# State-space scan with a mixture of experts: tokens routed first, a table of slots instead of sorted rows, experts from tile 8

## What is computed

```python
delta = softplus(xn @ W_delta.T + delta_bias)            # [token, d]
B_sel, C_sel = xn @ W_B.T, xn @ W_C.T                    # [token, d, n], n = 16
A_bar = exp(delta * A);  h = A_bar * h + (A_bar - 1) / A * B_sel * x   # along the 2048 tokens
y = sum over n of h * C_sel
...
scores = xf @ Wr + br                                    # 8 experts, the best 2 of each token
router_weights = softmax over the chosen two
h = gelu(xf @ W1[e] + b1[e]);  y = h @ W2[e] + b2[e]     # hidden size 1024
out = sum over e of router_weights[t, e] * y[e, t]
```

## Time and profile before

| | us |
|---|---|
| median of three runs (1290.12 to 1294.3) | 1290.58 |
| the profiled execution | 1290.72 |
| its span, first to last instruction | 1289.0 |
| prologue, to the start of the scan stage | 103.41 |
| PE / DVE / ACT / POOL busy | 1174.5 / 977.8 / 803.8 / 835.1 |

### The profile page before, as it was taken

One profiled execution on the slowest core, in us unless ns is written; L12 is line 12 of the kernel. 1 busy time (PEld: TensorE's weight loads), 2 busy tenths in 40 slices (PEclk: granted clock), 3 DMA queues, 4 the chain that ended last, 5 costly groups with the idle time before them and its releaser, 6 DMA issues.

```text
span 1289.0 us, 22376 instructions
## 1 busy us (share of the span) xinstructions
PE 1174.5 (91%) x7674; PEld 730.4 (57%) x7674; DVE 977.8 (76%) x1362; ACT 803.8 (62%) x1341; POOL 835.1 (65%) x733
## 2 busy tenths in 40 slices
PE   1467887789899999999999999999999999999996
PEld 0342333455556666666666666666666666666652
DVE  6767998887777777777776866767777776776788
ACT  3553445577788775666567567576756657566631
POOL 2536788357878676665766676666675766667662
PEclk9998989999999999999999999999999999999998
DMA  9942234667768753445344354344444354334423
GB/s 295 301 126 103 80 107 141 229 209 233 260 210 270 235 139 111 119 102 141 104 111 131 93 138 131 90 121 134 105 124 122 100 136 119 107 114 105 103 62 138
DMA packets 87387, 186.96 MB, mean 145 GB/s; under 512 B 12784, under 2 KB 64880, under 8 KB 77168
## 3 DMA queue, kind: packets, MB, share of 16 engines
q1 hardware_dynamic: 59280, 152.80, 35.3%
q0 software_dynamic: 18000, 22.42, 10.6%
q10 hardware_dynamic: 10000, 10.38, 3.3%
HBM read 135.48 MB, written 57.96 MB: 150 GB/s over the span
## 4 chain that ended last, share of the span: by engine, by line
PE 72%; POOL 6%; DVE 6%; issue 5%; ACT 2%; DMA 1%; DVEq 0%; SPq 0%; POOLq 0%; ACTq 0%
PE bank L1165 39%; PE bank L1214 15%; PE bank L1227 15%; POOL xs L953 3%; DVE hb L1069 3%; POOL ax L938 2%; PE bank L1194 1%; PE bank L1239 1%; DVE bank L1047 1%; POOL whl L948 1%; DMA wst<-in_W 1%; DVE bank L1081 1%; PE bank L1246 1%; DVE ysum L1090 1%; DVE bank L1043 0%
## 5 line engine op out<-in xcount | busy, mean ns | idle before, releaser
L938 POOL TENSOR_TENSOR ax<-ax,x 128x512 f32<-128x512 f32 x214 | 272.1, 1279 | 287.2 <-ACT ax L843 285.2
L1165 PE MATMUL bank<-k_xT,k_WB 128*128 128x512 f16 x1536 | 379.5, 384 | 47.2 <-DVE hb L1069 34.4
L1165 PE MATMUL bank<-k_xT,k_WC 128*128 128x512 f16 x1536 | 377.0, 382 | 0.8 <-DVE ysum L1090 0.8
L1047 DVE TENSOR_TENSOR bank<-ax,bank 128x512 f32<-128x512 f32 x214 | 148.4, 693 | 222.9 <-PE bank L1165 197.9
L1165 PEld LDWEIGHTS bank<-k_xT,k_WB 128*128 128x128 f16 x1536 | 146.2, 99 | 200.8 <-DVE hb L1069 51.2
L1165 PEld LDWEIGHTS bank<-k_xT,k_WC 128*128 128x128 f16 x1536 | 151.4, 99 | 186.3 <-issue 7.2
L1069 DVE TENSOR_TENSOR_SCAN hb<-aexp,state,bank 128x512 f32<-128x512 f32 x192 | 244.4, 1273 | 0.0
L833 ACT ACTIVATE aexp<-k_dcur,k_A 128x512 f32<-128x512 f32 x256 | 180.8, 711 | 72.1 <-DVE hb L1069 66.8
L1214 PE MATMUL bank<-xbt,k_x 128*128 128x256 f16 x1872 | 218.7, 274 | 3.8 <-ACT k_x L881 3.8
L1214 PEld LDWEIGHTS bank<-xbt,k_x 128*128 128x128 f16 x1872 | 183.8, 98 | 42.9 <-ACT k_x L881 4.8
L1081 DVE SCALAR_TENSOR_TENSOR bank<-hb,k_rA,bank 128x512 f32<-128x512 f32 x240 | 179.9, 749 | 1.8
(11 more groups left out here) (144 smaller groups left out, 1321.6 us busy)
## 6 DMA issues: line engine op xcount, KB each, us to landing
k_x<-wsplit SPq DMA_DIRECT2D x78, 1024.0 KB, 4.8
wst<-in_W SPq DMA_DIRECT2D x32, 512.0 KB, 5.8
wsplit<-whl SPq DMA_DIRECT2D x32, 512.0 KB, 5.6
xs<-zero ACTq DMA_DIRECT2D x1, 10140.0 KB, 61.1
xb<-xs SPq DMA_DIRECT2D x39, 260.0 KB, 4.5
b<-in_b SPq DMA_DIRECT2D x39, 128.0 KB
k_x<-in_x SPq DMA_DIRECT2D x4, 1024.0 KB, 9.7
stB<-in_WBT SPq DMA_DIRECT2D x8, 512.0 KB, 10.0
```

Of the source, the lines that this page charges most:

```text
L938: nc.gpsimd.tensor_tensor(ax[:, k % MR], ax[:, k % MR], x32[:], ALU.mult).then_inc(ax_done, 1)
L1047: v.tensor_tensor(bank, ax[:, RANK[g] % MR], bank, ALU.mult).then_inc(ux_done, 1)
L1165: ins = mm(bank[:], W[:, a, kc, n, hf * P:(hf + 1) * P], xT[:, c, b, kc, :], start=(k == 1), stop=(k == 3 * KC))
```

## The change

- **Prologue**: unrolled, with x's chunks and the scores first and the weight groups between and after them. The low half of W_B is made by DVE for groups 0, 6 and 7 and by POOL for the others (then ACT needs two operations for W_B, too). Scores of the high and low half of Wr come from one matmul of 16 columns.
- **Slot masks**: a token's slot is split into slot div 128 and slot mod 128. DVE compares both with 0..77 and 0..127 (two operations of 2496 elements per partition, four of 2048), POOL multiplies the first kind by the token's number (two of 2496), and PE multiplies the masks (64 matmuls of 78 columns): the result says which token is in each slot. From it DVE makes `row`, `second` and `target` for all blocks at once.
- **No `xs`**: the zeros and the 64 scatters go. SP writes all normalised rows with two extra columns to `xrows` (4.2 MB, two DMAs) once the gates are known, between weight groups 4 and 5. POOL gathers each block with two indirect DMAs. DVE's `slot_marks` and half of POOL's `slot_data` go.
- **Experts by size**: the experts take their places in order of their number of tokens, so that place p is not needed before block 4p. Two of the 32 weight pieces are split in the prologue, two at tiles 1 and 3, then one in every block.
- **Schedule**: blocks begin at tile 8, four of 7 tiles, then of 6; the last one ends at tile 246 (before: 239). The down product is spread over all tiles of a block from its third on (4 or 5 parts). `DIRECT` is cut to tiles 1, 3, 5, 7. Result rows are added to `acc` after each half of D (15 adds in place of 7), `take_y` of the last block is at tile 252 (before: 244).

In order: the tables of the schedule; in the prologue SP's, ACT's and DVE's programs (the last behind `slotf`); in the scan stage POOL's.

```diff
-E0 = 36
-EARLY, LONG, STEP = E, 6, 5
-DOWN_CUT = (0, 6, 11, 16)
-DIRECT = set(range(1, block_start(EARLY), 2))
-PIECE_AT = {k: E0 - 18 + 4 * k if k < 4 else block_start((k - 4) // 4) + 3 + k % 4 for k in range(SPLITS)}
+E0 = 8
+LONG, STEP, LONGS = 7, 6, 4
+def block_start(b):
+    return E0 + LONG * min(b, LONGS) + STEP * max(b - LONGS, 0)
+def down_steps(b):
+    return list(range(block_start(b + 1) + 2, block_start(b + 2)))
+def down_part(b, k):
+    n = len(down_steps(b))
+    return DOWN[k * len(DOWN) // n:(k + 1) * len(DOWN) // n]
+DIRECT = set(range(1, 8, 2))
+AHEAD = 2
+PIECE_AT = {2: 1, 3: 3, **{k: block_start(k - NPIECE) + 3 for k in range(NPIECE, SPLITS)}}
...
+        for g in range(4):
+            load_group(g)
...
+        load_group(4)
+        sp.wait_ge(meta_set, 1)
+        sp.dma_start(io["xrows"][0:HOLE, :].rearrange("(i p) d -> p i d", p=P),
+                     xall[:, 0:NT // 2, :]).then_inc(keep["rows_out"], 16)
...
+        for g in range(5, NG):
+            load_group(g)
+        sp.wait_ge(order_set, 1)
+        sp.wait_ge(table_made, 1)
+        for k in range(W_BUF):
+            load_piece(sp, io, keep, k)
+        for k in range(AHEAD):
+            store_piece(sp, io, keep, k)
+            load_piece(sp, io, keep, k + W_BUF)
...
-        act.dma_start(io["xs"].rearrange("(p r) d -> p r d", p=P),
-                      zero[:].unsqueeze(1).broadcast_to([P, NSLOT // P, D + META])).then_inc(keep["zeros_out"], 16)
...
+        ch.run(v.tensor_scalar(slot_hi[:], slotf[:], 1.0 / P, -(P / 2 - 0.5) / P, ALU.mult, ALU.add))
+        ch.run(v.tensor_scalar(slot_hi[:], slot_hi[:], ROUND, -ROUND, ALU.add, ALU.add))
+        ch.run(v.scalar_tensor_tensor(slot_lo[:], slot_hi[:], -float(P), slotf[:], ALU.mult, ALU.add))
+        for k in range(2):
+            v.tensor_tensor(hot_hi[:, k], slot_hi[:, k].unsqueeze(2).broadcast_to([P, NT, NS]),
+                            lane_ps[:, 0:NS].unsqueeze(1).broadcast_to([P, NT, NS]), ALU.is_equal).then_inc(hi_made, 1)
...
+        dve.sem_inc(meta_set, 1)
+        for k in range(2):
+            for h in range(2):
+                half = slice(h * NT // 2, (h + 1) * NT // 2)
+                v.tensor_tensor(hot_lo[k][:, half], slot_lo[:, k, half].unsqueeze(2).broadcast_to([P, NT // 2, P]),
+                                lane_ps.unsqueeze(1).broadcast_to([P, NT // 2, P]), ALU.is_equal).then_inc(lo_made, 1)
...
-        def scatter(j):
-            i, k = j // 2, j % 2
-            nc.gpsimd.indirect_dma_start(
-                out=io["xs"], out_offset=bass.IndirectOffsetOnAxis(keep["slot"][:, k, i:i + 1], 0),
-                in_=xrows[:, i], in_offset=None).then_inc(scattered, 16)
+        def gather(b):
+            if b >= 2:
+                pool.wait_ge(turn_made, USE["turn", b - 2] + 1)
+                pool.wait_ge(w_set, b - 1)
+            for s in range(BS):
+                at = b * BS + s
+                nc.gpsimd.indirect_dma_start(
+                    out=xb32[:, b % 2, s], out_offset=None, in_=io["xrows"],
+                    in_offset=bass.IndirectOffsetOnAxis(keep["row"][:, at:at + 1], 0)).then_inc(xb_in[b % 2], 16)
...
+                if block_start(b) + 4 == g and b + 2 < NBLK:
+                    gather(b + 2)
```

More of the change, by code:

```diff
@@ L69, in run @@
         self.eng.wait_ge(self.sem, self.n)
[L72 to L82, removed]
@@ L85, in softplus_parts @@
[L85 to L99, removed]
@@ L523 @@
-SLOT_DATA_AT = {block_start(b) + 5 + (b < EARLY): b for b in range(NBLK)}
-DIRECT = set(range(1, block_start(EARLY), 2))
+TAKE_Y_AT = {g + 1: b for g, b in DOWN_END.items()}
+DIRECT = set(range(1, 8, 2))
 SPLIT_TILES = [g for g in range(TILE_N) if g not in DIRECT]
@@ L594, in adds_before @@
     for g in range(TILE_N + 8):
-        for c in range(NCH - 1):
-            if row_add_step(c) == g:
-                count["row", c] = n
-                n += 1
+        if g - 3 in ROW_AT and ROW_AT[g - 3][0] < NCH - 1:
+            count[("row",) + ROW_AT[g - 3]] = n
+            n += 1
         if g - 3 in TAKE_Y_AT:
@@ new lines, in place_of, with project_z @@
+def place_of(eng, keep, b):
+    return bass.ds(eng.value_load(keep["eblk"][0:1, b:b + 1], min_val=0, max_val=E - 1), 1)
+def expert_of(eng, keep, b):
+    return bass.ds(eng.value_load(keep["eid"][0:1, b:b + 1], min_val=0, max_val=E - 1), 1)
+def project_z(nc, keep, out, c, done):
+    for hf in range(KC):
+        k = 0
+        for kc in range(KC):
+            for a, b in ((0, 0), (0, 1), (1, 0)):
+                k += 1
+                ins = nc.tensor.matmul(out[hf][:], keep["Wd"][:, a, kc, hf * P:(hf + 1) * P],
+                                       keep["xT"][:, bass.ds(c, 1), b, kc, :].squeeze(1),
+                                       start=(k == 1), stop=(k == 3 * KC))
+    ins.then_inc(done, 1)
@@ new lines, in softplus_parts @@
+def softplus_parts(nc, act, keep, src, z_ready, z_count, chain, chain_at, taken, ln_done):
+    act.wait_ge(z_ready, z_count)
+    for hf in range(KC):
+        bias = keep["dbias"][:, hf:hf + 1]
+        nc.scalar.activation(keep["zt"][:, hf], src[hf][:], ACT.Abs, scale=1.0 / WSCALE, bias=bias).then_inc(chain, 1)
+        ins = nc.scalar.activation(keep["rel"][:, hf], src[hf][:], ACT.Relu, scale=1.0 / WSCALE, bias=bias)
+        if taken is not None:
+            ins.then_inc(taken, 1)
+    act.wait_ge(chain, chain_at + KC)
+    nc.scalar.activation(keep["zt"], keep["zt"], ACT.Exp, scale=-1.0).then_inc(chain, 1)
+    act.wait_ge(chain, chain_at + (KC + 1))
+    nc.scalar.activation(keep["zt"], keep["zt"], ACT.Ln, bias=1.0).then_inc(ln_done, 1)
@@ L902, in _ @@
                     exp_tile(g - 1 + LEAD)
[L903 removed]
+            for k in range(AHEAD, SPLITS):
                 if PIECE_AT[k] == g:
[L905 removed]
+                    scale_piece(nc, act, keep, k)
             if g >= 1 and (g - 1) // TILES % RCH != RCH - 1:
@@ L913, in _ @@
                 less_one(g + MR - 1)
-            for k in range(SPLITS):
+            for k in range(AHEAD, SPLITS):
                 if PIECE_AT[k] == g:
-                    high_piece(k)
+                    high_piece(nc, act, keep, k)
     @block.gpsimd
@@ L1015, in _ @@
             if g == 0:
-                pool.wait_ge(keep["zeros_out"], 16)
-            for k in range(SPLITS):
+                gather(1)
+            for k in range(AHEAD, SPLITS):
                 if PIECE_AT[k] + 3 == g:
-                    low_piece(k)
-            if g < NT:
-                scatter(2 * g)
-                scatter(2 * g + 1)
+                    low_piece(nc, pool, keep, k)
             b, q = HIDDEN_AT.get(g - 4, (None, None))
```

1067 lines of the change are left out of this document (547 added, 520 removed).

## The result

The changed kernel takes **1320.22 us** (median of 4 runs, 1319.07 to 1321.23) against 1290.98 for the kernel before on the same chip: ratio 1.0221, interval 1.02 to 1.0242. It is slower; the forecast was 1271.2 with a range up to 1288. The profiled execution took 1319.07 us with a span of 1317.1, so 2.0 us lie around it.

| stretch | forecast | measured | off |
|---|---|---|---|
| start to barrier | 122.8 | 139.4 | +16.6 |
| barrier to scan 8 | 33.0 | 35.6 | +2.6 |
| scan 8 to scan 246 | 1070.1 | 1099.5 | +29.4 |
| scan 246 to the end | 43.6 | 42.6 | -1.0 |
| span | 1269.5 | 1317.1 | +47.6 |

The account below looks back on a forecast made before the run. PE was taken to bound the middle, DVE's pace the first 36 and some 14 last tiles, after a 103.41 us prologue. 122.8 + 33.0 + 1062.1 + 8 + 43.6 = 1269.5, with 1.7 around it 1271.2 us; range 1255 to 1288.

Parts of the forecast that it names:

- The row adds in halves, gathers and marks change nothing on PE: Scan stage: the split result-row adds, gathers and marks were to add no PE time, 0 us in the sum.
- the 8 us of stalls and their bound of 20: Tile 8 to 246: 8 us added for PE waiting on singly placed weight pieces, bounds 0 and 20.
- PE's 27.1 us: Scan stage: PE's work for six tiles and a block, against about 22 for ACT and 23.8 for POOL.
- The rival in which POOL is the bound: Scan stage: gathers of 3.6 us each make POOL slower than PE, blocks 29.0 us, total 1309; chance 0.08.
- the forecast's own signs of being wrong: Barrier below 116 or above 130 us; blocks over 28 us; PE waiting for POOL or ACT in them.
- with some ten small operations (0.25 each) the gates are ready at 83.5 us: Prologue: DVE's small operations follow the first two masks, done at 80.9 us, and finish the gates at 83.5.
- the scores' chain: Prologue: DVE's chain from scores at 61.0 us to slot cast, 12.6 as before; with reordering and slot splitting 74.9.
- The write as the plug of SP's queue: Prologue: the 4.23 MB row write, taken as 14 us, holds back weight groups 5 to 7; group 5 lands at 102.0.
- The end: Tile 246 to the end: late output copies set the length, 43.6 us, where DVE's own path gives 39.1.
- The gain between scans 8 and 246: Scan stage: 1062.1 us of PE work plus 8 of stalls, against 1116.4 before; 46.3 won.
- the 0.9 us that the forecast booked for the scatters left out: Barrier to tile 8: 16 scatters go, two pieces come, DVE keeps its pace; 33.0 us against 33.9 before.
- so DVE keeps up in each: Tile 8 to 246: light tiles carry 12 down-product matmuls and last 3.9 us; DVE needs about 3 per tile.

## Why the prediction was wrong

**The step that failed most: "The row adds in halves, gathers and marks change nothing on PE"**, and with it the 8 us of stalls and their bound of 20. The forecast counted POOL's operations per block and found them under PE's 27.1 us, which they are: 20.74 us busy in block 34 that lasts 29.40. It did not ask in which order POOL stands and what it waits for. The change made 14 row adds of 7 (L1073 x14; of the 15 halves turned, one goes out with the last rows), and nine of them fell where the rows come late from PE and the block add follows directly. Two waits of up to 4.7 us in a row then stood in front of `times_x`. 25 us, shown by moving the add (25.8), leaving it out (26.6) and moving the turn (25.4). A sign of it stood in the earlier trace rows: with seven row adds, the block add (L990) already waited 6.2 us for `acc<-base`. The rival in which POOL is the bound had the right engine, sign and about the right time (1309), but its mechanism, slow gathers, didn't happen: 1.01 us against its 2.65. Two of the forecast's own signs of being wrong came: a barrier above 130 us, and blocks of over 28 us.

**The second: "with some ten small operations (0.25 each) the gates are ready at 83.5 us"**. They took 11.5 us, not 2.5 (from 88.7 to the gates at 100.2), because four of them waited for POOL. The forecast looked at whether the masks are disturbed, and they aren't, but put the masks ahead of the small operations without seeing that the masks *start* POOL's two multiplications of 4.35 us, beside which all the small ones then run. The same holds for the scores' chain, taken from the earlier trace rows where it ran without POOL's low halves: five operations (L604, L605, L607, L609, L637) lost 1.4 to 2.1 us each, 8.4 in all. 9.0 and 8.4, less 0.6 for the quicker masks, are the 16.7 us, to 0.1. The waits are shown by the gates put first (8.9 of their 14.1 us) and by the operands in PSUM, where the same operations beside the same work of POOL take their short times; putting the router there won 5.5 us.

This sign, too, stood in the rows of before. In the earlier trace rows the cast L451, of 64 elements, starts at 98.37 and takes 1.77 us. Beside it runs this product:

```profile
97.40 2.69 POOL L281 TENSOR_TENSOR k_dcur<-rel,zt 128x1024 f32<-128x1024 f32 x1 [15.43 <-ACT zt L99]
```

It ends at 100.09 us, the cast at 100.14, where the other operations of 64 elements take 0.2 with POOL idle: already before the change a small operation had waited for the rest of a long one of POOL.

The Trainium skill (SBUF — State Buffer, Who interferes with whom) says that a VectorE operation with two inputs in SBUF contends with a GpSimd operation that reads SBUF, that copy, cast and tensor_scalar can take the shared ports, too, and that the other then blocks wholly. The trace agrees in each: two inputs in SBUF 4.29 us, one in PSUM 0.22, tensor_scalar 4.18, cast 1.74, copy 2.05. The forecast used this rule for the large operations and not for the small ones.

**What was right.** The write as the plug of SP's queue: gates to barrier 39.2 us against 39.3. Masks 2.7 against 3.0. The end: 42.6 against 43.6, with `take_y` 19.3 us after scan 246 and the copy's landing 21.5 behind it (forecast 19.6 and 22.0). The gain between scans 8 and 246: 46.3 us forecast, 43.2 once the row add had its place. With both faults and the write's queue mended the kernel takes 1276.65, 5.4 over the forecast, and its stretches are 122.9, 35.6, 1073.2 and 43.1 us against 122.8, 33.0, 1070.1 and 43.6. That the first agrees to 0.1 is chance: the chain up to the slots is still 8.4 us longer than forecast, and the gates no longer stand behind the masks (5.4 us), nor the loads behind the write: the errors cancel.

**Smaller misses.** From the barrier to scan 8 it took 35.6 us for 33.0. 1.4 of the 2.6 stand before the first scan, which comes 7.0 us behind the barrier (5.6 before): POOL issues block 0's two gathers from 140.18 to 142.61, ahead of its first product, and DVE waits for that product until 145.25. The tiles behind it go at 3.57 us where the kernel before had 3.53, so the 0.9 us that the forecast booked for the scatters left out didn't come.

Block 0 is 4.0 us over PE's work. The forecast had down parts in every light tile ("so DVE keeps up in each"), but block 0 has none, as no block stands before it: its five light tiles last 3.45 to 3.56 us, where PE needs 2.59 and then waits for DVE's scan, 0.69 us at a time in three of them.

**Open.** Why blocks 1 and 3 are 1.8 and 1.9 us over PE's work wasn't taken apart (both have a delta product in their first tile; without sevens and with the delta products moved, no block but block 0 is over 0.1 us too long, and that one 3.1). What the scatters, the direct tiles and the spread of the weight pieces are worth singly is not known.

## What to carry to other kernels

A queue's load per block says little about an engine that also waits: for each DMA that is issued from a computing engine, write down what it waits for, how late that can be where it now falls, and what is issued next behind it. An accumulating DMA directly ahead of another to the same tensor costs its landing, here up to 4.7 us; with two tiles between them, the block's add first, it cost nothing. And before an operation of POOL is started, finish DVE's short chain that others wait for, or keep one of the two inputs in PSUM, in every operation of the chain, as the next one takes up the wait: a 0.2 us operation beside a 4.35 us one of POOL took up to 4.3 us. Whether an operation with a single input is free when that lies in PSUM no run here shows.

## What the runs showed of the hardware

- A small operation of DVE beside one of POOL lasted until POOL's ended: 64 elements with two inputs in SBUF 4.29 us, 32 elements with one input, in SBUF, 4.18, against 0.23 and 0.18 with POOL idle. Reductions beside POOL's work (0.21 us at 88.7, 0.22 at 95.0) and two-input operations with one input in PSUM (0.22) did not wait.
- An issue behind a DMA of 2 MB can hold its queue: the second write 4.47 us on ACT's (1.99 on SP's), and on SP's the 512 KB load behind the two writes 6.87 us; it landed 15.9 us after its issue began.
- In the changed kernel the accumulating DMA of the rows landed 4.6 to 6.5 us after its issue, 5.1 in the median.
- Loads beside a large write on another queue are slower, but not stopped: weight pieces landed 9 us after issue in place of 4.5.
